# First attention batch prepared during the third group of the first layer, its projections placed among the last group's gates, and SBUF buffers laid out by lifetime

## The reference

```
# layer 0: gated recurrent update with cross attention
tok    = ctx @ W_proj + b_proj
attn   = softmax(x @ tok^T / sqrt(256));  routed = attn @ tok
ps_n   = ln(x) * g_state + beta_state;    in_n = ln(routed) * g_input + beta_input
u      = sigmoid([ps_n, in_n] @ W_u + b_u);  r = sigmoid([ps_n, in_n] @ W_r + b_r)
cand   = tanh([r * ps_n, in_n] @ W_n + b_n)
x1     = ln((1 - u) * x + u * cand) * g_out + beta_out
# layer 1: transformer block, 16 heads of 64
h  = ln(x1, ln1);  x2 = attention(h, h, a1) + x1        # self attention
h  = ln(x2, ln2);  x3 = attention(h, ctx, a2) + x2      # cross attention
h  = ln(x3, ln3);  out = (u * gelu(gate)) @ ff_Wo + ff_bo + x3
```

## Time and profile before

| what | us |
|---|---|
| median of 3 runs (1081.17 to 1081.41) | 1081.24 |
| the profiled execution | 1081.92 |
| its span from first to last instruction | 1080.1 |
| TensorE busy in the span | 988.0 |
| VectorE busy | 712.8 |
| ScalarE busy | 625.8 |
| GpSimd busy | 356.5 |

### The profile page before, as it was taken

How to read it: one execution, slowest core, us unless ns; L and a number is a source line. 1 busy time by engine, 2 the same in 40 slices (tenths; PEclk the granted TensorE clock), 3 DMA queues, 4 the chain that set the end, 5 groups by cost and what they waited for, 6 DMA issues and landing times.

```text
span 1080.1 us, 21165 instructions
## 1 busy us (share of the span) xinstructions
PE 988.0 (91%) x7776; PEld 927.1 (86%) x7776; DVE 712.8 (66%) x1610; ACT 625.8 (58%) x1945; POOL 356.5 (33%) x474
## 2 busy tenths in 40 slices
PE   4688775499999999999999999999999998899998
PEld 4577654389999999999989889999999998899998
DVE  3466745496767666767667885776677667666664
ACT  2566443286657565657566765766676667534343
POOL 1101323133333333333342343554454454401010
PEclk9999888699999999999999998999999999999999
DMA  6221000100300000000000300300000001000100
GB/s 206 68 68 34 26 20 20 44 11 2 97 3 21 1 21 1 22 1 21 2 21 2 103 18 9 104 25 2 25 26 10 17 21 58 12 30 21 41 30 20
DMA packets 30444, 34.60 MB, mean 32 GB/s; under 512 B 4360, under 2 KB 23816, under 8 KB 30344
## 3 DMA queue, kind: packets, MB, share of 16 engines
q1 hardware_dynamic: 30344, 33.26, 10.2%
HBM read 24.86 MB, written 8.39 MB: 31 GB/s over the span
## 4 chain that ended last, share of the span: by engine, by line
PE 77%; DVE 10%; ACT 7%; issue 2%; POOL 1%; DMA 1%; SPq 1%; DVEq 0%; POOLq 0%
PE bank L1324 14%; PE bank L1325 14%; PE bank L1326 14%; PE bank L1549 8%; PE bank L1532 5%; PE bank L1336 5%; PE bank L1590 3%; PE bank L1591 3%; PE bank L1592 3%; PE bank L1564 3%; ACT p L737 2%; PE bank L1440 1%; PE bank L1506 1%; DVE bn L903 1%; DVE hT_lo L1089 1%
## 5 line engine op out<-in xcount | busy, mean ns | idle before, releaser
L737 ACT ACTIVATE p<-bank,negmax 128x256 f32<-128x256 f32 (+1 forms) x512 | 208.2, 428 | 18.4 <-DVE negmax L1106 15.5
L554 POOL TENSOR_TENSOR oT_hi<-oT,ones 128x256 fp32r<-128x256 f32 x128 | 93.7, 732 | 370.7 <-DVE oT L1129 370.7
L747 ACT CAST pT_hi<-bank 128x512 fp32r<-128x512 f32 (+1 forms) x256 | 110.8, 486 | 166.1 <-PE bank L1549 165.9
L1324 PE MATMUL bank<-hT_hi,w_hi 128*128 128x256 f32 x640 | 190.8, 298 | 6.3 <-DVE hT_lo L1089 2.5
L1326 PE MATMUL bank<-hT_hi,w_lo 128*128 128x256 f32 x640 | 181.6, 284 | 0.0
L1325 PE MATMUL bank<-hT_lo,w_hi 128*128 128x256 f32 x640 | 181.4, 283 | 0.0
L1324 PEld LDWEIGHTS bank<-hT_hi,w_hi 128*128 128x128 f32 x640 | 122.7, 192 | 9.9 <-DVE hT_lo L1089 4.8
L1121 DVE TENSOR_TENSOR pT_lo<-bank,pT_hi 128x512 fp32r<-128x512 f32 (+1 forms) x256 | 129.9, 550 | 0.5
L1102 DVE TENSOR_REDUCE negmax<-bank 128x2 f32<-128x512 f32 x128 | 82.2, 684 | 66.8 <-PE bank L1532 66.8
L1325 PEld LDWEIGHTS bank<-hT_lo,w_hi 128*128 128x128 f32 x640 | 123.1, 192 | 0.0
L1326 PEld LDWEIGHTS bank<-hT_hi,w_lo 128*128 128x128 f32 x640 | 122.8, 192 | 0.0
(11 more groups left out here) (202 smaller groups left out, 2737.8 us busy)
## 6 DMA issues: line engine op xcount, KB each, us to landing
w_stage<-in_weights SPq DMA_DIRECT2D x47, 256.0 KB, 4.5
x_in<-x_dram SPq DMA_DIRECT2D x24, 256.0 KB, 2.9
x_dram<-x_out SPq DMA_DIRECT2D x16, 256.0 KB, 3.2
l_x<-in_x SPq DMA_DIRECT2D x4, 512.0 KB, 5.0
x_dram<-l_out SPq DMA_DIRECT2D x4, 512.0 KB, 2.8
out_dram<-x_out SPq DMA_DIRECT2D x8, 256.0 KB, 3.1
w_stage<-in_weights SPq DMA_DIRECT2D x9, 128.0 KB, 5.1
l_ctx<-in_ctx SPq DMA_DIRECT2D x4, 180.0 KB, 4.4
```

Of the source, the lines that this page charges most:

```text
L554: nc.gpsimd.tensor_tensor(oh[:, G % PAIRS, :], of[:, :], ones[:, :], ALU.mult).then_inc(y["o_hi"], 1)
L737: last = nc.scalar.activation(p[:, G % 2, e, t * cols:(t + 1) * cols], scores_at(G, e, t), ACT.Exp, bias=negmax[:, G % 2, t, e:e + 1], acc ...
L747: nc.scalar.copy(pTh[0:r, G % 2, e, 0:n], bank[4 + e][0:r, 0:n]).then_inc(y["pT_hi"], 1)
L1324: nc.tensor.matmul(dst, lh, rh, start=(i == 0), stop=False)
```

## The change

The first layer's last group becomes a function of its own on three engines (`last_group`), and the steps that begin the attention layer move into it and into group 2. The wait for all four groups is gone.

- SyncE stores group 0 and loads attention batch 0 straight away; the context load, store 1 and `load(1)` follow, then stores 2 and 3, then `load(2)`.
- VectorE makes batch 0's statistics, normalised form and gains in group 2, ahead of that group's new state. `prepare_lo(0)`, `self_low(0, 0)`, the eighth weight unit and the context's split stand in the last group.
- TensorE transposes batch 0 behind the first part of the last group's gate r, moves the state part of gate u ahead of `routed_T`, and puts the projection of pair 0 behind it. `context(B)` stands before `new_T(2)`; pairs 1 and 2 and the first values follow the last gate at once; `new_T(3)` stands ahead of the first scores. The transposes of the last group go to banks 6 and 7 (they were 1 and 3), and the first projections use banks 2, 5, 4 and 3.
- GpSimd's `gain_out` becomes eight operations over 256 columns in every group. The sixteen memsets of the v buffers move to it from VectorE. Its list has the last group's `out_scale`, then step 0, then the last `gain_out`.
- The buffers of both layers are declared in a new order so that those alive together lie apart; the statistics of the attention layer have buffers of their own (`mean_var_h`, `bn_h`, `rstd_h`).

No matmul is added or taken away. The diff, cut to its core (all of GpSimd, SyncE, then ScalarE, VectorE and TensorE):

```diff
+        def out_banks(it):
+
+            return (6, 7) if it == LAST else (1, 3)
...
-            for it in range(NI):
-                store_first(it)
-            sp.wait_ge(z["stored"], 16 * (NI + 1))
...
+            store_first(0)
+            sp.wait_ge(z["stored"], 16 * 2)
             load(0)
+            sp.wait_ge(z["xhat"], NI)
+            sp.wait_ge(z["xT"], NI)
             load_context(B)
+            store_first(1)
             load(1)
+            store_first(2)
+            store_first(3)
+            sp.wait_ge(z["stored"], 16 * (NI + 1))
             load(2)
...
                 pool.wait_ge(z["ohat"], it + 1)
                 if it == 0:
                     pool.wait_ge(z["rows_in"], 16 * len(ROWS))
-                nc.gpsimd.tensor_tensor(x1o[:, :, :], x1o[:, :, :],
-                                        row("L0_xattn_g_out").unsqueeze(1).broadcast_to([128, L0T, D]),
-                                        ALU.mult).then_inc(z["scaled"], 1)
+                for t in range(L0T):
+                    last = nc.gpsimd.tensor_tensor(x1o[:, t, :], x1o[:, t, :], row("L0_xattn_g_out"), ALU.mult)
+                last.then_inc(z["scaled"], 1)
                 pool.wait_ge(z["scaled"], it + 1)
-                nc.gpsimd.tensor_tensor(x1o[:, :, :], x1o[:, :, :],
-                                        row("L0_xattn_beta_out").unsqueeze(1).broadcast_to([128, L0T, D]),
-                                        ALU.add).then_inc(z["out"], 1)
+                for t in range(L0T):
+                    last = nc.gpsimd.tensor_tensor(x1o[:, t, :], x1o[:, t, :], row("L0_xattn_beta_out"), ALU.add)
+                last.then_inc(z["out"], 1)
 
             def out_scale(it):
...
                     out_scale(it - 1)
                 if front:
+                    if it + 1 == LAST:
+                        inverse_std(0)
                     routed_scale(it + 1)
+                if it == LAST:
+                    add_bias(0)
+                    pool.wait_ge(z["rps"], KT * NI)
+                    for v_ in (vh, vl):
+                        for pr in range(PAIRS):
+                            last = nc.gpsimd.memset(v_[:, :, pr * VW + DH:pr * VW + 2 * DH].bitcast(F32), 0.0)
+                    last.then_inc(zeros_ready, 1)
                 if it >= 1:
                     gain_out(it - 1)
...
+                if G == PAIRS // 2:
+                    pool.wait_ge(z["stored"], 16 * (NI + 1))
...
+            def first_constants():
+                nc.gpsimd.memset(ones[:, :], 1.0).then_inc(neg_half_ready, 1)
+                pool.wait_ge(neg_half_ready, 2)
+
+            state_scale(0)
+            full_xT(0)
+            routed_scale(0)
+            for it in range(NI):
+                first_layer(it)
+            first_constants()
+            out_scale(LAST)
+            step(0)
+            gain_out(LAST)
+            for G in range(1, STEPS):
                 step(G)
...
+            def last_group():
+
+                prepare(0)
+                routed_gains(LAST)
+                act.wait_ge(z["xT_full"], NI)
+                round_self(0, 0)
+                reset_tanh(LAST)
+                weights_hi(act, 8)
+                round_context(B)
+                update_tanh(LAST)
+                candidate_tanh(LAST)
+                normalise_out(LAST - 1)
...
+            last_group()
+            round_self(0, 1)
+            round_self(0, 2)
             round_values(0, 0)
-            round_self(0, 1)
             softmax_pair(0)
             round_values(0, 2)
-            round_self(0, 2)
-            for G in range(STEPS // 2):
+            step_self(0)
+            normalise_out(LAST)
+            for G in range(1, STEPS // 2):
...
+                lo_tokens(it + 1)
+                lo_reset(it)
+                if it >= 1:
+                    out_stats(it - 1)
+                lo_pT(it + 1)
+                kept_state(it)
+                if it < 2:
+                    for n in (WCHUNKS[0] + 2 * it, WCHUNKS[0] + 2 * it + 1):
+                        weights_lo(dve, n)
+                if before_last:
+                    prepare_stats(0)
+                lo_state(it + 1)
+                routed_stats(it + 1)
+                if it + 2 < NI:
+                    lo_context(it + 2)
+                if before_last:
+                    prepare_xhat(0)
+                    prepare_full(0, 4)
+                new_state(it)
...
+            def last_group():
+
+                prepare_lo(0)
+                lo_routed(LAST)
+                self_low(0, 0)
+                reset_product(LAST)
+                lo_reset(LAST)
+                weights_lo(dve, 8)
+                context_low(B)
+                out_stats(LAST - 1)
+                kept_state(LAST)
+                new_state(LAST)
...
-            for v_ in (vh, vl):
-                for pr in range(PAIRS):
-                    last = nc.vector.memset(v_[:, :, pr * VW + DH:pr * VW + 2 * DH].bitcast(F32), 0.0)
-            last.then_inc(zeros_ready, 1)
...
+            last_group()
+            self_low(0, 1)
+            self_low(0, 2)
             values_low(0, 0)
-            self_low(0, 1)
             row_max(0)
             values_low(0, 2)
-            self_low(0, 2)
+            out_stats(LAST)
...
+            def last_group():
+
+                gate_r_state(LAST)
+                prepare(0, 4)
+                gate_u_state()
+                routed_T(LAST)
+                project_self(0, 0)
+                gate_r_routed(LAST)
+                pe.wait_ge(y["h_full"], KT)
+                context(B)
+                new_T(LAST - 1)
+                gate_u_routed()
+                gate_n_routed(LAST)
+                gate_n_reset(LAST)
...
+                if G == 0:
+                    pe.wait_ge(z["tanh_u"], KT * NI)
+                    pe.wait_ge(z["ohat"], LAST)
                 if 1 <= G < STEPS // 2:
...
                 if G == 0:
                     pe.wait_ge(zeros_ready, 1)
+                    pe.wait_ge(z["ohat"], NI)
...
                 pe.wait_ge(y["h_split"], b + 1)
-                if PAIRS * b + g >= 1:
-                    pe.wait_ge(y["qk_lo"], PAIRS * b + g)
                 if b == 0 and g == 0:
                     pe.wait_ge(w_ready, 8)
+                elif b == 0 and g == 2:
+                    pe.wait_ge(z["tanh_u"], KT * NI)
+                elif b == 0 and g == 3:
+                    pe.wait_ge(y["v_lo"], value_product(0, 2))
+                else:
+                    pe.wait_ge(y["qk_lo"], PAIRS * b + g)
                 h = hidden(b)
                 for i, w in enumerate((A1W + "q", A1W + "k")):
...
+                if b == 0 and c == 0:
+                    pe.wait_ge(y["cT_lo"], 1)
+                elif b == 0 and c == 2:
+                    pe.wait_ge(z["ohat"], LAST)
+                else:
...
+            last_group()
+            project_self(0, 1)
+            project_self(0, 2)
             project_values(0, 0)
-            project_self(0, 1)
+            new_T(LAST)
             scores(0)
             project_values(0, 2)
```

376 lines of the change are left out of this document (176 added, 200 removed).

## The result

The changed kernel takes **1040.3 us** (median of four runs, 1037.26 to 1043.19) against 1081.2 before: ratio 0.9624, interval 0.9597 to 0.965. The direction was right; 1051 and the range from 1043 to 1059 were not. The kernel gained 40.9 us where 30.4 were forecast. Two further sets of runs of the same kernel (e4 and e18), each beside the kernel before on its own chip, gave 1041.94 and 1038.02.

A forecast was written before the change was run, and what follows sets the result against it. TensorE, busy 91% of the span, was taken as the bound, with gains in the low-clock first eight slices. 31.1 + 3.0 - 3.7 = 30.4 us off 1081.2 gave 1051 us, range 1043 to 1059.

The forecast's parts named there:

- TensorE's work between the two starts: Matmuls and transposes from gate r of the last group to the projection of pair 3: 30.6 us.
- The wait behind routed_T(3): TensorE waits for hT_lo before projecting pair 0, as five VectorE operations take 1.25 each beside GpSimd: 3.9 us.
- The clock there: Lower TensorE clock after the wait for hT_lo, over pair 0's projection and a gate part: 3.6 us, bounds 0 and 4.5.
- the small waits: Scores 1 waiting for pair 0's first exp, and pair 3 for v's low half: 0.7 us.
- the stretch: Gate r of the last group to the projection of pair 3: 38.8 us against 69.9, a gain of 31.1.
- The start of group 2: Shorter VectorE collisions with GpSimd there start the next gate r 3.0 us earlier, bounds 0 and 6.
- The first steps: Attention's first steps, where out_stats(3) and gain_out(3) now stand ahead of other work: loss 3.7 us, bounds 2 and 8.
- a sign against it: Forecast wrong if TensorE waits for GpSimd or a DMA between 144 and 200, or later time differs beyond 3.7 us.
- GpSimd's queue and the memsets: Sixteen v-buffer memsets on GpSimd at 0.3 each, 4.8 us, ahead of the last group's gains; no loss expected.
- the cover: Slack between GpSimd's store, done at 185, and the last l_out that wants it at 188: 3 us.
- the clock holds: Rival: VectorE slips through more often, wait 2.1, no low clock in either place, 1046 us; chance 0.20.
- The other rivals: VectorE shut out, 1055 us (0.16); GpSimd's queue late, 1057 (0.15); slower, 1084 (0.02); change does nothing, 1081 (0.01).

The follow-up runs named there:

- e4: The changed kernel run again unaltered, beside the kernel before on its own chip: 1041.9 us (1040.5 to 1045.5).
- e18: The changed kernel run once more unaltered, beside the kernel before on its own chip: 1038.0 us (1036.0 to 1041.7).
- e3: The changed kernel with an unused buffer declared at 48 bytes in each partition ahead of the layers' buffers: 1048.9 us.
- e10: The changed kernel with an unused buffer of 64 bytes ahead of the layers' buffers: 1049.0 us.
- e1: The kernel before with only its SBUF buffers declared in the changed kernel's order, every instruction as it was: 1072.1 us against 1081.5.
- e7: The changed kernel with batch 0's hT_lo ahead of the four l_cand on VectorE, and the last group's routed transposes between gate u's halves on TensorE: 1041.5 us.
- e16: The changed kernel with out_stats(3) behind the row maxima of step 1 on VectorE and gain_out(3) behind widen_sums(1) on GpSimd: 1041.9 us against 1038.0.
- e12: The kernel before with 32 unused bytes ahead of everything, the weights included: 1081.6 us, ratio 1.0004.

## Why the prediction missed, by its steps

- **TensorE's work between the two starts**, 30.6: right. In e18 it is 30.77 busy at full clock, with no other step in it.
- **The wait behind routed_T(3)**, 3.9: it was 2.56 (2.58 in e18, 3.14 in e4). In the profiled run the term was mis-sized by 1.3. The collisions cost 1.1 to 1.2 each, near the 1.25 taken, but only for four of the five operations: the first `l_cand`, at 149.97, slipped in at 0.68. The gains, taken as of fixed length, stretched in return: four took 4.46 beside VectorE's two-input operations, where the same four took 2.80 in the next group without them.
- **The clock there**, 3.6: mis-sized by 2.1. The projection took 0.4 longer and gate r 1.1 longer, since the low clock began in the middle of the projection and ended inside gate r (back near 159.8). In e18 it cost nothing; in e4 it was at 0.50 throughout 153 to 159. The two terms and the small waits (0.46 against 0.7) make the stretch 35.1 instead of 38.8.
- **The start of group 2**, 3.0: 1.4 at gate r in the profiled run, 4.0 and 4.9 in the two others, inside its bounds. `l_cand` was right (1.26, 1.22). The wait for `l_xT_lo` vanished altogether, since TensorE reached it late: it had run the products ahead of it at half clock, from 112.0 to 115.4, behind a wait of 1.78. The low clock only moved from behind the scores to ahead of them. In the profiled run the errors of the modelled steps (3.7 us too dear in the stretch and 0.3 behind it, 1.6 too cheap here) partly cancel.
- **The first steps**, 3.7: 3.4 in the profiled run, with waits of 2.03, 0.73 and 0.73. The last is a wait for GpSimd at 194.92, inside the stretch where the prediction counts any such wait as a sign against it; its own term for `widen_sums(1)` had one there.
- **GpSimd's queue and the memsets**: sixteen took 2.45 us, 0.15 each, half the price taken; the cover held. While they ran, `l_cand` took 0.69 and 0.68, against 1.67 beside the `x_plus_bias` ahead of them. The rule weighed in the prediction (the Trainium skill, "SBUF — State Buffer", section "Who interferes with whom": a write-only GpSimd instruction doesn't block VectorE) agrees with this trace.
- **The step that failed** is one that the prediction took at nothing, without a reason, and then put among its marks of failure: that behind the first steps all runs as before. It read the diff's "buffers laid out by lifetime" as having no price. The lead grew there by 5.9 us; e3 and e10, the changed kernel at the pace of before, took 1048.9 and 1049.0, inside the forecast's own bounds of 1048 to 1054. The layout alone gave 9.3 on before (e1). In medians, of the 40.9 us some 32 belong to the moved steps (1081.2 to 1049) and some 9 to the layout (1049 to 1040.3). This is what put the result outside the range.
- The rival "the clock holds", 1046, held in e18 in part, behind a wait of 2.58 where it had 2.1. Its own terms give 1044, not 1046: with the wait at 2.1 instead of 3.9 another 1.8 comes back. The other rivals didn't occur.

What stays open: by which rule the distance sets the pace, why runs at equal addresses lie up to 1 ns apart (e1 and the changed kernel), and what decides in a single run whether the clock falls behind a wait of 2.6 us.

## What to carry to other kernels

A change that declares buffers in another order has a price of its own, in the whole kernel: compare the start-to-start time of matmuls in a part that wasn't edited before crediting the edit, and try a few pads between weights and activations when TensorE is the bound. Take the distances from the built program and not from the declared sizes: here pads that were not multiples of 32 bytes were rounded up, and two pairs of runs tried one layout twice. A GpSimd operation that VectorE must sit out can be cut into pieces, which pays where VectorE is on the path. A wait removed from a tight chain of four engines came back twice (e7, e16) as the next one: walk the list past the wait before counting its length as gain.

## What the hardware did that I had not expected

- Moving the activations by 32 bytes against the weights (e2) changed the time from one feed-forward matmul to the next by 2% (122.2 to 120.0 ns), moving both (e12) changed nothing; the best pace measured was 118.3 (e1), 3.1% below.
- After a wait of 2.56 us the granted clock fell to 0.50 in one run, and after one of 2.58 it stayed at 1.00 in another of the same kernel. It fell behind 1.78 us too (after, 0.50 from 112.0 to 115.4), and held behind 2.12 (before, at 76.04). At the turn near 650, behind waits of 2.24 and 2.30, it was 0.58 over 10 us before, with 52 matmuls, and 1.00 in e1, with 84.
- GpSimd and VectorE that read SBUF at the same time slow each other: beside VectorE's two-input work four gains took 4.46 us, against 2.80 at best.
